# ScalarE takes a batch's exponentials in the slot of its scores, behind two copies, in a gated cross-attention and expert kernel

## What is computed

```python
x = x + tanh(g_xattn[0]) * xattn(ctx_1024, layernorm(x))     # x: 128 batches of 64 rows of 128
x = x + tanh(g_ffn[0]) * ffn(layernorm(x))                   # 8 experts, 2 chosen for each row

# in xattn, for each batch: 8 heads, 64 queries, 128 keys (64 of the context, 64 of x itself)
sim  = einsum('bhid,bhjd->bhij', q * DH ** (-0.5), k)
attn = softmax(sim, axis=-1)
out  = einsum('bhij,bhjd->bhid', attn, v)
return out.transpose(0, 2, 1, 3).reshape(b, -1, INNER) @ Wo + bo
```

## Time and profile before

| | us |
|---|---|
| runs, all three | 797.94, 799.97, 800.05 |
| median | 799.97 |
| span of the profiled execution, first to last instruction | 795.7 |

### The profile page before, as it was taken

How to read it: one execution, slowest core, us unless ns; L and a number is a source line. 1 busy time by engine, 2 the same in 40 slices (tenths; PEclk the granted TensorE clock), 3 DMA queues, 4 the chain that set the end, 5 groups by cost and what they waited for, 6 DMA issues and landing times.

```text
span 795.7 us, 17460 instructions
## 1 busy us (share of the span) xinstructions
PE 760.7 (96%) x5392; PEld 643.6 (81%) x5392; DVE 528.3 (66%) x1829; ACT 496.9 (62%) x1630; POOL 446.1 (56%) x455
## 2 busy tenths in 40 slices
PE   7999999999999999999999999999999999979788
PEld 6778777777888988778988878898877888868765
DVE  5636677685857567677658776776868567565536
ACT  3677777676766566766656667565567665554522
POOL 2233264646552544785655586665568566556664
PEclk9999999999999999999999999999999999999999
DMA  7735151542454642174754226664414555634523
GB/s 198 209 150 194 60 213 69 211 146 81 145 188 154 205 153 72 38 231 143 237 189 143 65 76 218 206 212 163 127 54 140 180 191 188 212 112 116 154 77 87
DMA packets 119791, 119.42 MB, mean 150 GB/s; under 512 B 14585, under 2 KB 94994, under 8 KB 119698
## 3 DMA queue, kind: packets, MB, share of 16 engines
q1 hardware_dynamic: 111088, 102.41, 39.1%
q0 software_dynamic: 7680, 15.74, 6.8%
q10 hardware_dynamic: 930, 0.15, 0.1%
HBM read 35.94 MB, written 41.55 MB: 97 GB/s over the span
## 4 chain that ended last, share of the span: by engine, by line
PE 77%; issue 6%; POOL 6%; DVE 5%; ACT 4%; DMA 1%; another core or an unknown queue 1%; SPq 1%; POOLq 0%; ACTq 0%; DVEq 0%
PE shared L1426 13%; PE batch L1364 11%; PE batch L1377 11%; PE hid_ps L1294 8%; PE xy_ps L1308 7%; PE batch L1372 6%; PE shared L1217 3%; PE shared L1219 3%; PE shared L1218 3%; ACT probs L746 3%; PE batch L1308 2%; POOL probs L676 2%; PE xy_ps L1271 2%; POOL yg L666 2%; PE batch L1354 2%
## 5 line engine op out<-in xcount | busy, mean ns | idle before, releaser
L676 POOL TENSOR_TENSOR probs<-probs,rsums 128x512 f32<-128x512 f32 x128 | 132.9, 1039 | 231.7 <-DVE rsums L1147 230.1
L746 ACT ACTIVATE probs<-batch,neg_max 128x128 f32<-128x128 f32 x512 | 180.5, 374 | 2.0 <-DVE neg_max L1151 2.0
L651 POOL DMA_INDIRECT sorted_x<-xn,row_of x120 | 124.4, 1036 | 33.6 <-issue 28.7
L827 ACT ACTIVATE qT<-shared,tb 128x512 f32<-128x512 f32 x128 | 87.2, 696 | 85.6 <-PE shared L1219 72.4
L1377 PE MATMUL batch<-pT_sb,kvn 128*128 128x512 f32 x256 | 133.7, 604 | 2.9 <-ACT pT_sb L754 2.9
L1364 PE MATMUL batch<-kvT,qT 128*128 128x128 f32 x1024 | 135.4, 275 | 0.8 <-ACT qT L827 0.8
L1426 PE MATMUL shared<-M,oT 128*128 128x128 f32 x1024 | 125.5, 276 | 0.3
L1364 PEld LDWEIGHTS batch<-kvT,qT 128*128 128x128 f32 x1024 | 124.4, 192 | 1.2 <-ACT qT L827 1.2
L1426 PEld LDWEIGHTS shared<-M,oT 128*128 128x128 f32 x1024 | 119.4, 192 | 1.6 <-issue 1.6
L746 ACT ACTIVATION_READ_ACCUMULATOR probs<-batch,neg_max 128x1 f32 x512 | 110.2, 215 | 0.0
L1147 DVE RECIPROCAL rsums<-sums 128x4 f32<-128x4 f32 x128 | 22.7, 178 | 130.4 <-ACT probs L746 119.9
(11 more groups left out here) (168 smaller groups left out, 1243.4 us busy)
## 6 DMA issues: line engine op xcount, KB each, us to landing
wt<-wall SPq DMA_DIRECT2D x124, 321.0 KB
sorted_x<-yg SPq DMA_DIRECT2D x36, 512.0 KB, 4.8
xt<-sorted_x SPq DMA_DIRECT2D x162, 64.0 KB
sorted_y<-y_sb SPq DMA_DIRECT2D x78, 128.0 KB
kv<-in_ctx_dram SPq DMA_DIRECT2D x16, 256.0 KB
kv<-in_x_dram SPq DMA_DIRECT2D x16, 256.0 KB
xres<-in_x_dram SPq DMA_DIRECT2D x32, 128.0 KB
out_dram<-x SPq DMA_DIRECT2D x15, 256.0 KB
```

The source lines that it names most:

```text
L651: nc.gpsimd.indirect_dma_start(xs[k % SETS][:, :], bass.IndirectOffsetOnAxis(ap=row_of[:, g, choice, c:c + 1], axis=0), xn[:, g % 2, c, :] ...
L676: nc.gpsimd.tensor_tensor(pv, pv, rsums[:, m % 2, :].unsqueeze(2).broadcast_to([P, 4, P]), ALU.mult).then_inc(probs_ready, 1)
L746: last = nc.scalar.activation(probs[:, m % 2, c * P:(c + 1) * P], batch_ps[m % BANKS][:, c * P:(c + 1) * P], ACT.Exp, bias=neg_max[:, m % ...
L827: nc.scalar.activation(qT[:, g % 2, :, number, :], sh[:, :].rearrange("p (b i) -> p b i", b=GB), ACT.Identity, bias=tb[:, number:number + ...
```

## The change

ACT's slot n held the copy of a product (batch n - 3), the exponentials of batch n - 1 and the copy of turned probabilities (batch n - 2), in this order. It now holds the copy of a product, the copy of turned probabilities, and the exponentials of batch n, whose scores PE multiplies in this same slot. Nothing else is edited: the constant `EXP = 1` still sets the slot of DVE's reciprocals and of POOL's multiplication.

```diff
             def slot(n):
                 if 0 <= n - OUT - 1 < B:
                     keep_product(n - OUT - 1)
-                if 0 <= n - EXP < B:
-                    exponentials(n - EXP)
                 if 0 <= n - TURN < B:
                     keep_turned(n - TURN)
+                if 0 <= n < B:
+                    exponentials(n)
                 g = n // GB - 1
```

## The result

The changed kernel takes 820.47 us (median of four runs, 819.33 to 821.74) where the kernel before takes 798.96 in the runs beside it: a ratio of 1.0275, 95% interval 1.0262 to 1.0289. It is slower, as predicted, but by 21.5 us and not by 4, and it lies outside the range of 792 to 811. One run of E9 (4348.8 us) and one of the kernel before, beside E5 to E8 (1090.0 us), were in a slow state, and the ratios leave them out.

The account below looks back on a forecast made before the run. TensorE, busy for 96% of a 795.7 us span, was taken as the bound. 17 us of added waits less 13 saved gave +4, on the 799.97 median 804.0 us; range 792 to 811 for 8 in 10.

Parts of the forecast that it names:

- With a tile the same shift is covered: Slots with an expert tile: moved exponentials leave the product's copy in time by over a microsecond, so no loss.
- Place 7 into place 0: Lean (tile-free) slots: place 0's projection waits for the product's copy, 0.97 late; eight times, one at 0.46, 7.3 us.
- Place 2: Lean slots: the projection waits for the product's copy behind place 1's exponentials and key copies, 1.04 late eight times, 8.3 us.
- much slower: Rival: late projections delay DVE's next reduction and lateness goes round in places 0 and 2; 8 us more, 812; chance 0.08.
- Places 4 and 6: Lean slots: place 4's projection 0.46 late in slots 4, 20 and 28, 1.4 us together; place 6 stays as it is.
- limit of 0.76: A projection is late once the product's copy ends more than 0.76 us after the scores' start.
- The saved side: Lean slots: TensorE's waits for turned probabilities, POOL's multiplication, logits and projection read-out shrink, 6 + 4 + 2 + 1 = 13 us.
- The copy of turned probabilities: Lean slots: this copy goes ahead of the exponentials, so the product no longer waits; 6 us saved, between 2.9 and 10.8.
- the logits: Lean slots: DVE gets to the logits sooner, so TensorE waits less; 2 us saved, between 1.1 and 6.9.
- faster: Rival: saved waits go and new ones don't come, or only half; 787 us with none, 795.5 with half; chance 0.22.
- A copy of `xtT` too late for the hidden layer: Sign of being wrong: a tile's stretch becomes longer because ScalarE copies the turned tile late; no size given.
- the limit of the gain: Whole kernel: savings are cut by TensorE's idle time, 35.0 us in all, 6.1 of it in slots 0 to 42.

Follow-up runs that it names:

- E9: The changed kernel, but in place 1 of groups without a tile ScalarE copies place 2's product right behind the exponentials, ahead of two key read-outs: 813.05 us, ratio 1.0225.
- E5: The change only in places 0, 2, 4, 5 and 6 away from tiles; elsewhere exponentials stay a slot later, as in the kernel before: 785.77 us, ratio 0.9851.
- E8: The changed kernel, but in place 1 of groups without a tile the exponentials stay a slot later, as before: 808.11 us, ratio 1.0140.
- E2: The change only in slots with a tile and those next to one; other slots keep the order of the kernel before: 808.25 us, ratio 1.0137.
- E3: The changed kernel, but ScalarE copies the turned tile (xtT) ahead of the exponentials, for tiles sharing slots with the attention: 814.44 us, ratio 1.0209.
- E7: E3's edit on the changed kernel, and in place 7 of every group the exponentials stay a slot later: 798.39 us, ratio 1.0030.
- E4: The changed kernel, but in place 7 of groups without a tile the exponentials stay a slot later, as before: 803.40 us, ratio 1.0075.
- E10: The changed kernel, but in place 7 of groups without a tile ScalarE takes two query read-outs ahead of the exponentials: 812.43 us, ratio 1.0208.
- E6: The kernel before with the copy of turned probabilities ahead of the exponentials, which stay a slot later than their scores: 820.58 us, ratio 1.0294.
- E11: E9's copy ahead, with the exponentials a slot later in places 3 and 7 and in or next to tile slots: 788.94 us, ratio 0.9901.

## Why the prediction was wrong

**What fell: "With a tile the same shift is covered".** It was priced at 0, and it is 12.2 us of the 22.8 (10.4 in E2, where slot 96 is only 0.3 longer). The prediction followed one instruction behind the exponentials, the product's copy, in one slot. `xtT` stands behind them too, TensorE's next output waits for it, and the tile's own matmuls, taken as the cover, are the work that is held up. E2 shows the loss alone, and E3 and E7 that most of it goes with that copy's place (places 0 to 6: 11.2 to 2.4 and to 1.0).

**Place 7 into place 0: right chain, wrong waiter.** The prediction ended the read-outs of queries at 4.97 into slot 23 and asked only when the next product's copy would follow. But slot 24's scores wait for these read-outs, and slot 23 was 3.70 long: by its own numbers they are 4.97 - 3.70 = 1.27 late, eight times, 10.2 us. Measured are 1.25 of wait in slot 24, and 10.3 + 0.9 us in places 7 and 0, where 7.3 was written. E4 shows the cause; E10 shows the term as it was written (6.3 us), which appears when the earlier waiter is served.

**Place 2: right, with a size too small.** Predicted 1.04 eight times, 8.3; slot 26 shows a wait of 0.95 and is 1.19 longer, and all nine slots of place 2 sum to 11.2. E8 shows that place 1's exponentials cause it. What was missing is mostly slots 66 and 90 (2.0 and 1.9 longer), where the slot ahead had become 1.4 us shorter, and slot 2 (0.8). Slot 2 has no projection; there the copy of turned probabilities stands behind slot 1's key copies, and the product waits for it:

```profile
35.81 0.70 PE L1377 MATMUL batch<-pT_sb,kvn 128*128 128x512 f32 x1 [0.81 <-ACT pT_sb L754]
```

The rival "much slower", lateness that goes round, is not shown: at most it is the 2.0 us by which places 1 and 2 together fall in E4, not 8.

**Places 4 and 6.** Predicted 0.46 in each of slots 4, 20 and 28; these are 0.74, 0.71 and 0.71 longer, and savings in the other slots of place 4 leave 0.7 of it. In slots 20 and 28 this was luck: the sum took 3.70 for the slot ahead, but slots 19 and 27 took 4.42 and 4.19, so by its own limit of 0.76 the copy would have been in time (4.92 - 4.42 = 0.50 in slot 20); it comes late because the change makes them 0.85 and 0.61 shorter. In E8, where they save nothing, slots 20 and 28 lose 0.1 and 0.3. Place 6, predicted unchanged, is 0.4 longer, all of it in slot 6.

**The saved side.** 13 predicted, 3.5 + 2.1 + 7.8 = 13.4 in the lengths of places 1, 3 and 5: right in sum, but not by its terms. The copy of turned probabilities was priced at 6 us and the logits at 2; in slot 21 the product starts 2.48 after the scores in place of 2.87, which is 0.39 of the 0.92 that the slot wins, and the rest comes behind the product, where the second query waited for the logits. E6 shows that the exchange of order alone brings none of it.

**The sum.** Lean +10.1 in place of +4, tile +12.2 in place of 0, start and end +0.6. The rival "faster" is refuted for the change as a whole: none of the places with a new wait was spared, though in place 0 another waiter hid it. The two effects can be had apart, as E5 shows. A copy of `xtT` too late for the hidden layer was named in the prediction as a sign that it was wrong, without a price or a chance; it came true, for the output of the tile before.

## What to carry to other kernels

When an instruction that must wait is moved on an in-order engine, list everything that stands behind it there, in every kind of slot, and carry the new time to the first waiter of each, the next slot's included; a cover checked for one of these copies says nothing of the others. Saved and added waits mostly lie in different places, so work out the balance by place, and make the change only where it is positive: here that turned +2.75% into -1.5%. The places are not independent: a slot that a saved wait makes shorter brings the next one forward, and a copy that was in time there can be late (slots 20, 28, 66 and 90).

## What the runs showed of the hardware

**Busy time of TensorE held waits.** E5 shortens slots 0 to 42 by 187.29 - 180.65 = 6.6 us, more than the 6.1 that PE was idle there before; its busy time itself falls by 181.20 - 176.75 = 4.5 us for the same work. One such case is the product of slot 23, whose row is 1.12 us long before, where it came close behind the copy of turned probabilities, and 1.02 in E5. The prediction took PE's idle time as the limit of the gain. To this extent the measurement sides with the Trainium skill (Perfetto Trace Analysis, "Identifying the Most-Contended Engine"), which calls matmul busy time a bad measure of how close a kernel is to the roofline; the share of weight loads, one of the two measures that it names instead, is not tested by this.

**A wait costs more than its idle time.** In the changed kernel the scores take 1.16 us in the nine slots in which they waited for `qT`, and 1.06 in 118 of the other 119.

**The clock fell right after slot 0 in three traces.** In the trace after the granted clock was 0.50 (1.2 of 2.4 GHz) from 29.6 to 33.0; PE had been idle for 0.78 us ahead of slot 0's scores and had then multiplied 16 single columns. The same work stood there before, at 1.00. Rows by busy time as above, first after, then before:

```profile
29.90:32.10 2.20, 2.20 (x11) 2.20 (x12) 1.75 (x10) 0.61 (x4) 0.35 (x1) 0.50 0.20 61
```

```profile
31.00:33.20 2.20, 2.20 (x21) 2.09 (x20) 2.13 (x11) 1.31 (x7) 0.00 (x0) 1.00 0.00 0
```

Slot 1's scores took 2.06 us there in place of 1.14. In E3 and E6 the same scores were long too (1.55 and 2.05), in the other experiments they were not. Slots 0 and 1 together are 0.6 us longer than before, which bounds its part in the 22.8; its cause stays open.

**It fell ahead of slot 0 in two others.** In the kernel before it was 0.50 from 13.0 to 16.4, and in E11 from 12.4 to 15.8; PE had been idle for 1.39 and 1.12 us shortly before. E5 has 1.35 us of idle time at the same place and keeps 1.00. Eight transposes of keys (L1415) took 1.92 us there before, and 1.07 in E5 (L1423). These two traces reach slot 0's scores last, at 28.55 and 29.02; the other eleven do at 26.67 to 27.64. So the trace before has a slow start, and the trace after, 1.5 us sooner at slot 0, does not owe that to the change.
